# Three score units instead of two in a block of values, in the last two stretches of an attention and mixture-of-experts kernel

## The chip, the cores and the metric

The kernel runs on one core of one Trainium2 chip. The metric is the device time of one execution in microseconds (us). Three runs of the kernel before gave 296.19, 296.71 and 296.82 us: the median is 296.71 us. The execution that was profiled took 296.31 us, and its span, from the first to the last instruction, is 294.6 us.

## What is computed

The reference is one transformer layer on a single sequence, x of shape (1, 2048, 128) in fp32:

```python
x = x + _L0_attn_ref(_layernorm(x), w_qkv, w_out)
x = x + _L0_ffn_ref(_layernorm(x), base_W, base_b, shared_A, shared_B,
                    routed_A, routed_B, router_W, router_b)
```

The attention has 16 heads of 8 dimensions each, rotary embedding on queries and keys, a causal mask and a softmax over the keys:

```python
scores = jnp.einsum('bhqd,bhkd->bhqk', q, k) * scale
scores = jnp.where(causal, scores, jnp.finfo(scores.dtype).min)
out = jnp.einsum('bhqk,bhkd->bhqd', jax.nn.softmax(scores, axis=-1), v)
```

The feed-forward part adds a dense 128x128 layer, a shared low-rank pair (rank 16) and six routed low-rank pairs (rank 16), of which each token takes the two with the highest gate; the gates are a softmax over six logits, kept for those two and normalised again.

## The kernel before

**Stretches.** Queries are handled in six pieces of 2 or 4 tiles of 128 rows, `PIECES` = (0,2) (2,2) (4,4) (8,4) (12,2) (14,2), as (first tile, tiles). The text calls the time of a piece a stretch, numbered 0 to 5; the last two are stretches 4 and 5, each with 256 queries. In every stretch the 16 heads are taken in four groups of four, one group after the other.

**Score units.** The work of a group is a list of units, numbered through the whole kernel from 0 to 279. In a stretch of two tiles a unit is "wide" (one tile of 128 keys against 256 queries, four heads, 1024 scores in each of 128 partitions) or "half" (the last diagonal tile, 128 queries, 512 scores in a partition). The stretches begin at units 0, 8, 24, 76, 160 and 216. Stretch 4 has 14 units for each group and stretch 5 has 16, the last diagonal tile (the half unit) at the end of each group; only in the very last group the two diagonal tiles come first. So the half units of the last two stretches are 173, 187, 201, 215, 231, 247, 263 and 265.

For each unit TensorE computes the scores (L1198) into one of three slots of PSUM, `ps`; ScalarE takes the exponential of the whole slot (L758) into one of eight buffers in SBUF, `pbuf`; for diagonal units GpSimd sets the masked corner to zero (L685). The scores of unit n use the slot of unit n-3, so TensorE waits for the exponential of unit n-3 before them. The exponential of unit n waits until the block of values that reads the buffer of unit n-8 is done.

**Blocks of values.** The product of the exponentials with the values and a column of ones (L1223) is accumulated in one PSUM bank, `po`. `group_work` cuts the list of a group into blocks; a block's products are issued together, `LAG` = 5 units after its last unit. In stretches 4 and 5 a block is two wide or half units, and the last block of the kernel is cut into two of one unit. That makes 28 blocks in stretch 4 and 33 in stretch 5. After the last block of a group VectorE takes the sum out of `po` with a transpose (L831, `evacuate`), and the first block of the next group waits for that.

**Jobs.** All other work is cut into named jobs that are woven between the units: projections and splitting of queries and keys for later stretches, and the finish of a chunk of rows whose attention is done. The finish has eleven jobs: A (transpose), O (output projection and residual), M1 M2 M3 (layernorm), X (transpose), R (router and low-rank-down product), W1 W2 (choice of two routes), U (transpose of the gated low-rank rows), F (dense and up products, residual). O, X, R, U and F have a TensorE part (L1285, L1288, L1291, L1295, L1233 with L1299) and a VectorE part that reads it; R also has a small exponential on ScalarE (L766), which is placed in ScalarE's queue after the exponential of the unit that R is placed at, and waits for VectorE's logits (L984). U waits for VectorE's W2 and F for VectorE's copy of U. The chunks of rows are finished as c = 0 to 3 (4, 4, 4 and 2 tiles); the rows of the last two tiles are finished after the last unit by `end_of_chunk`.

**What sets the order.** Each engine has one queue in order, and the whole order is fixed by tables. `PLACES` gives, for each stretch, the unit (counted from the stretch's first) after whose scores each job comes. On TensorE the sequence at unit u is: the scores of u, the blocks of values that are due at u, the products placed at u. On VectorE it is: the evacuations due at u, the jobs placed at u. VectorE has no wait on a unit as such, so only the sequence of jobs and evacuations matters there. In stretches 0 and 1 the products of TensorE have places of their own (`SMALL_PLACES`), so `PLACES` moves only VectorE's jobs there. In what follows "O3 at 246" is the O product of chunk c = 3 placed at unit 246.

Of the kernel before, what the change touches and what calls it, by code (L numbers as in the profile page):

```python
# [73 lines left out]
NS_SMALL = 2  # L74
NPB = 8
LAG = 5


PREPS = ((0, 2), (2, 2), (4, 4), (8, 4), (12, 4))
PIECES = ((0, 2), (2, 2), (4, 4), (8, 4), (12, 2), (14, 2))  # L80
# [8 lines left out]
def group_work(t0, tiles, last):  # L89

    if tiles == 4:
        return ([[("full", kt, (0,)), ("full", kt, (1,))] for kt in range(t0 + 1)]
                + [[("ends", t0 + 1, (0,)), ("ends", t0 + 1, (1,))], [("mid", t0 + 2, (0, 1))]])
    wide = [("wide", kt, (0, 1)) for kt in range(t0 + 1)] + [("half", t0 + 1, (0, 1))]
    if last:
        wide = wide[-2:] + wide[:-2]
    return [wide[n:n + 2] for n in range(0, len(wide), 2)]


WOVEN = 1  # L100
# [7 lines left out]
def plan():  # L108


    units, blocks = [], []
    for i, (t0, tiles) in enumerate(PIECES):
        of_piece = []
        for g in range(NG):
            end = (i, g) == (NPIECE - 1, NG - 1)
            work = group_work(t0, tiles, end)
            if end:
                work[-1:] = [[unit] for unit in work[-1]]
            of_piece.append([(g, n, members, n == len(work) - 1) for n, members in enumerate(work)])
        if i == WOVEN:  # L120
            of_piece = [[one for both in zip(*of_piece[g:g + 2]) for one in both] for g in range(0, NG, 2)]
        for g, n, members, last in (one for group in of_piece for one in group):
            mine = list(range(len(units), len(units) + len(members)))
            for kind, kt, pairs in members:
                units.append(dict(i=i, g=g, kind=kind, kt=kt, pairs=pairs, diagonal=kt >= t0, block=len(blocks)))
            blocks.append(dict(i=i, g=g, units=mine, first=n == 0, last=last,
                               diagonal=any(units[u]["diagonal"] for u in mine)))
    return units, blocks
# [11 lines left out]
def blocks_by_unit():  # L140


    due = {}
    for b, block in enumerate(BLOCKS):
        due.setdefault(block["units"][-1] + LAG, []).append(b)
    return due


# [14 lines left out]
def value_terms(block):  # L163
# [49 lines left out]
    [(name, 2) for name in FINISH[FINISH_CUT:]] + [(name, 3) for name in FINISH],  # L213
)
PLACES = (
# [6 lines left out]
)  # L222


# [63 lines left out]
def build(nc, x, w_qkv, rope_c, rope_s, w_out, w_down, w_up, w_base, base_b, router_b, ident, head_sum,  # L288
# [3 lines left out]
    with ExitStack() as ctx:  # L292
# [487 lines left out]
        def _(dve):  # L780
# [384 lines left out]
            second_queries()  # L1165

            due = blocks_by_unit()
            for u in range(len(UNITS)):
                if u in FIRST_UNIT[1:] and FIRST_UNIT.index(u) in NEW_PREP:
# [4 lines left out]
                for n in JOBS_AT.get(u, ()):  # L1174
                    take(n)
            for u in range(len(UNITS), len(UNITS) + LAG):
                for b in due.get(u, ()):
# [5 lines left out]
        def _(pe):  # L1183
# [227 lines left out]
            pe.wait_ge(ones_set, 4)  # L1411
            pe.wait_ge(zeroed, 1)
            due = blocks_by_unit()
            for u in range(len(UNITS)):
                if u in FIRST_UNIT and FIRST_UNIT.index(u) in NEW_PREP:
# [13 lines left out]
                for name, c in PRODUCTS_AT.get(u, ()):  # L1429
                    job(name, c)  # L1430
            for u in range(len(UNITS), len(UNITS) + LAG):
                for b in due.get(u, ()):
# [59 lines left out]
```

## Time and profile before

| | us |
|---|---|
| median of three runs | 296.71 |
| profiled execution | 296.31 |
| its span | 294.6 |
| ScalarE busy | 268.9 (91%) |
| TensorE matmuls busy | 278.1 (94%) |
| VectorE busy | 138.6 (47%) |
| GpSimd busy | 65.5 (22%) |

The granted TensorE clock is at full speed (2.4 GHz) in every slice of the span. Instructions of ScalarE and TensorE are pipelined: a recorded duration can hold time in which the instruction waits behind the one before it, so a start is not always the true beginning, while an end is. For that reason this document counts with the ends of exponentials and with the distance from one matmul's start to the next one's start.

### The profile page before, as it was taken

How to read it: one execution, taken by the hardware profiler on the slowest of the kernel's cores; microseconds unless marked ns; L12 is line 12 of the kernel's file. 1: busy time of each engine (PE TensorE's matmuls, PEld its weight loads, DVE VectorE, ACT ScalarE, POOL GpSimd, SP SyncE). 2: the span in 40 equal slices, each digit the busy share in tenths (PEclk: the TensorE clock that was granted, in tenths of full speed). 3: DMA queues.
4: the chain of work that ended last, by engine and by line, in shares of the span. 5: the costliest groups of instructions: out<-in, count | busy, mean ns of one | idle time of the engine just before them, and what ended most of it. 6: DMA issues, size and time to landing. Idle time of an engine off the chain costs nothing.

```text
span 294.6 us, 7507 instructions
## 1 busy us (share of the span) xinstructions
PE 278.1 (94%) x2998; PEld 102.8 (35%) x2998; DVE 138.6 (47%) x419; ACT 268.9 (91%) x306; POOL 65.5 (22%) x139
## 2 busy tenths in 40 slices
PE   7979988999999999999999999999999999999996
PEld 2634332222222222132233134445433435444344
DVE  6875957686051558517171036522113262541055
ACT  8668899899999999999998999999999998999921
POOL 3647465423403021040030121010101010103002
PEclk9999999999999999999999999999999999999999
DMA  6343443004700000000001700001000000000000
GB/s 208 109 119 97 118 127 93 0 3 111 185 28 2 4 0 2 0 0 2 2 0 30 209 17 2 2 2 38 0 3 2 2 3 28 10 2 2 21 0 18
DMA packets 15400, 11.81 MB, mean 40 GB/s; under 512 B 2097, under 2 KB 14370, under 8 KB 15362
## 3 DMA queue, kind: packets, MB, share of 16 engines
q1 hardware_dynamic: 14738, 10.71, 13.1%
q8 instruction: 25, 0.41, 0.6%
q0 software_dynamic: 192, 0.39, 0.5%
q10 hardware_dynamic: 432, 0.20, 0.3%
q14 instruction: 13, 0.11, 0.1%
HBM read 3.95 MB, written 1.05 MB: 17 GB/s over the span
## 4 chain that ended last, share of the span: by engine, by line
PE 49%; ACT 26%; issue 14%; DVE 6%; DMA 2%; SPq 0%; ACTq 0%; DVEq 0%
ACT pbuf L758 26%; PE po L1223 22%; PE ps L1198 14%; PE pm L1239 1%; PE pm L1233 1%; PE pm L1285 1%; PE ps L1239 1%; PE ps L1347 1%; DMA qst<-parts 1%; PE pm L1245 1%; PE pm L1291 1%; PE pm L1299 1%; DMA xs<-x_dram 1%; DVE rest L851 1%; PE pm L1295 1%
## 5 line engine op out<-in xcount | busy, mean ns | idle before, releaser
L758 ACT ACTIVATE pbuf<-ps 128x1024 f32<-128x1024 f32 (+1 forms) x280 | 253.5, 1079 | 7.2 <-PE ps L1198 6.3
L1223 PE MATMUL po<-pbuf,va 128*9 128x256 f32 (+3 forms) x1792 | 143.8, 426 | 1.2 <-DVE oq L831 0.8
L1198 PE MATMUL ps<-qst,kst 64*128 64x256 bf16 (+3 forms) x896 | 97.3, 297 | 8.3 <-ACT pbuf L758 3.9
L685 POOL TENSOR_SCALAR_AFFINE_SELECT pbuf<-pbuf 128x256 f32<-128x256 f32 (+1 forms) x104 | 47.8, 482 | 194.1 <-ACT pbuf L758 193.7
L1198 PEld LDWEIGHTS ps<-qst,kst 64*128 64x128 bf16 x896 | 30.6, 94 | 106.8 <-ACT pbuf L758 80.3
L1223 PEld LDWEIGHTS po<-pbuf,va 128*9 128x9 f32 x1792 | 35.1, 89 | 55.4 <-issue 33.1
L831 DVE STREAM_TRANSPOSE oq<-po 128x256 f32<-128x256 f32 (+1 forms) x24 | 12.9, 539 | 66.4 <-PE po L1223 66.1
L851 DVE TENSOR_TENSOR rest<-pm,sinT 32x512 f32<-32x512 f32 x16 | 11.0, 687 | 0.3
L1347 PE MATMUL ps<-kst 128*128 128x512 bf16 (+1 forms) x38 | 9.8, 391 | 0.0
L798 DVE BATCH_NORM_STATS2 stats<-xs 128x6 f32<-128x128 f32 x32 | 7.1, 281 | 2.5 <-DMA xs<-x_dram 1.4
L1239 PE MATMUL ps<-xnT,wqkv 128*128 128x256 f32 (+1 forms) x24 | 8.0, 462 | 0.0
L999 DVE TENSOR_TENSOR xs<-pm,xs 128x512 f32<-128x512 f32 (+1 forms) x4 | 2.5, 624 | 11.1 <-PE pm L1299 11.1
L969 DVE TENSOR_TENSOR xs<-pm,xs 128x512 f32<-128x512 f32 (+1 forms) x4 | 2.5, 624 | 10.2 <-PE pm L1285 10.2
L1347 PE MATMUL ps<-xnT 128*128 128x512 bf16 x16 | 5.3, 508 | 1.5 <-DVE xnT L1129 1.5
L858 DVE TENSOR_TENSOR rot<-rot,rest 128x512 f32<-128x512 f32 (+1 forms) x10 | 6.4, 643 | 0.3
L996 DVE COPY lowT<-pm 113x512 f32<-113x512 f32 (+1 forms) x4 | 2.5, 625 | 8.5 <-PE pm L1295 8.5
L960 DVE COPY va<-pm 128x512 f32<-128x512 f32 x2 | 1.4, 692 | 10.8 <-PE pm L1245 10.8
L981 DVE TENSOR_TENSOR lg<-pm,rbias 128x24 f32<-128x24 f32 (+1 forms) x4 | 0.7, 180 | 12.1 <-PE pm L1291 12.1
L845 DVE TENSOR_TENSOR rot<-pm,cosT 128x512 f32<-128x512 f32 x4 | 2.8, 691 | 7.5 <-PE pm L1239 6.9
L634 POOL MEMSET qst<- 128x512 f32 (+1 forms) x9 | 6.0, 686 | 0.0
L701 ACT COPY kst<-fillers 128x2048 f32<-128x2048 f32 x3 | 5.7, 1897 | 0.0
L977 DVE COPY feat<-pm 128x512 f32<-128x512 f32 (+1 forms) x4 | 2.5, 625 | 6.4 <-PE pm L1288 6.4
(158 smaller groups left out, 189.5 us busy)
## 6 DMA issues: line engine op xcount, KB each, us to landing
qst<-parts SPq DMA_DIRECT2D x18, 128.0 KB, 2.6
kst<-parts SPq DMA_DIRECT2D x18, 128.0 KB, 2.4
xs<-x_dram SPq DMA_DIRECT2D x4, 256.0 KB, 3.2
cosT<-rope_c_dram SPq DMA_DIRECT2D x3, 256.0 KB, 3.8
sinT<-rope_s_dram SPq DMA_DIRECT2D x3, 256.0 KB, 4.1
out_dram<-xs SPq DMA_DIRECT2D x3, 256.0 KB, 2.3
kst<-parts SPq DMA_DIRECT2D x8, 64.0 KB, 2.4
qst<-parts SPq DMA_DIRECT2D x7, 64.0 KB, 2.0
```

Of the source, the lines that this page charges most:

```text
L634: nc.gpsimd.memset(stacked[:, :, first * P:(first + tiles) * P].bitcast(F32), value).then_inc(filled_by_pool, 1)
L685: ins = nc.gpsimd.affine_select(out=edge, in_=edge, compare_op=ALU.is_ge, fill=0.0, base=0, pattern=[[0, edge.shape[1]], [1, P]], channel_ ...
L701: nc.scalar.copy(kst[:, :, c * CH:(c + 1) * CH].bitcast(F32), fillers[:, 0:1].unsqueeze(2).broadcast_to([P, NP, CH // 2])).then_inc(filled, 1)
L758: nc.scalar.activation(probs[:, :, 0:width], ps[:, SLOT[u], :, 0:width], ACT.Exp, scale=SCALE).then_inc(exp_ready, 1)
L798: ins = nc.vector.bn_stats(stats[:, t, :], xs[:, tile + t, :])
L831: nc.vector.transpose(oq[:, g, mine, :].rearrange("p b r -> p (b r)"), po[:, output(i, g, 0, nt * P)]).then_inc(o_free, 1)
L851: ins = nc.vector.tensor_tensor(rest[there:there + HALF, which, cols], product[here:here + HALF, :], sinT[here:here + HALF, c % 2, cols], ...
L858: return nc.vector.tensor_tensor(rot[:, which, cols], rot[:, which, cols], rest[:, which, cols], ALU.add)
L1198: ins = nc.tensor.matmul(ps[:, SLOT[u], e, place:place + n], side(kst, e)[:, g * 2 + pair, key:key + P], side(qst, e)[:, g * 2 + pair, q:q ...
L1223: ins = nc.tensor.matmul(po[32 * j:32 * j + DH + 1, output(i, g, q0, n)], va[:, kt, g * GH + j, :], pbuf[:, u % NPB, at:at + n], start=blk ...
L1239: return nc.tensor.matmul(product, wqkv[:, which, :], xnT[:, chunk(p) % 2, local(p)], start=True, stop=True)
L1347: nc.tensor.matmul(into, left, right, start=True, stop=True)
```

## The change

A block of values in stretches 4 and 5 has up to three units in place of two; it is still issued five units after its last unit (the new `WIDE_LAG` has the value of `LAG`). That makes 20 blocks in stretch 4 (three, three, three, three and two units in each group) and 24 in stretch 5 (five of three units and one of one unit in each group). The last block of the kernel is then one unit, and the one before it three.

The places of jobs are changed in four of the six stretches. In stretch 0, K1 goes from 1 to 0, and in stretch 1, Q1 goes from 1 to 2. In stretch 4, W1 of chunk 1 goes from 24 to 27. In stretch 5 the finish of chunk 2 has W1, W2, U and F three units earlier, and the finish of chunk 3 has A, M1, M2, M3, X, R, W1, W2, U and F one to four units earlier; O stays. The products of TensorE that move are U2 (240 to 237), F2 (243 to 240), X3 (254 to 251), R3 (257 to 254), U3 (267 to 263) and F3 (270 to 266).

```diff
@@ -74,6 +74,8 @@
 NS_SMALL = 2
 NPB = 8
 LAG = 5
+WIDE_LAG = 5
+WIDE_BLOCK = 3
@@ -94,7 +96,8 @@
     wide = [("wide", kt, (0, 1)) for kt in range(t0 + 1)] + [("half", t0 + 1, (0, 1))]
     if last:
         wide = wide[-2:] + wide[:-2]
-    return [wide[n:n + 2] for n in range(0, len(wide), 2)]
+    size = 2 if t0 < 12 else WIDE_BLOCK
+    return [wide[n:n + size] for n in range(0, len(wide), size)]
@@ -142,7 +145,7 @@
     due = {}
     for b, block in enumerate(BLOCKS):
-        due.setdefault(block["units"][-1] + LAG, []).append(b)
+        due.setdefault(block["units"][-1] + (WIDE_LAG if PIECES[block["i"]][0] >= 12 else LAG), []).append(b)
     return due
@@ -213,12 +216,12 @@
 PLACES = (
-    (0, 0, 0, 1, 5),
-    (0, 1, 1, 3, 6, 6, 7, 11, 15, 15),
+    (0, 0, 0, 0, 5),
+    (0, 1, 2, 3, 6, 6, 7, 11, 15, 15),
     (6, 9, 10, 11, 12, 18, 22, 23, 25, 30, 34, 37, 40),
     (3, 3, 5, 8, 11, 19, 26, 31, 34, 34, 35, 39, 40, 44, 46, 50, 50, 51, 54, 61, 61, 62, 68, 72),
-    (7, 8, 10, 10, 12, 17, 19, 24, 27, 27, 33, 37, 40),
-    (3, 6, 9, 11, 15, 18, 21, 24, 27, 30, 30, 31, 35, 36, 38, 41, 44, 48, 51, 54),
+    (7, 8, 10, 10, 12, 17, 19, 27, 27, 27, 33, 37, 40),
+    (3, 6, 9, 11, 15, 15, 18, 21, 24, 27, 30, 30, 32, 33, 35, 38, 41, 45, 47, 50),
 )
```

## Rows read from the trace of the kernel before

**Rows 1.** Stretch 5: window, length, busy of PE PEld DVE ACT POOL, clock, DMA
```profile
222.80:281.40 58.60, 57.01 (x828) 25.47 (x823) 21.31 (x81) 56.86 (x65) 5.46 (x13) 1.00 0.03 9
```
**Rows 2.** ScalarE's timeline, units 150 to 279: start, length to last end, what
```profile
161.24 27.42 ACT L758 ACTIVATE pbuf<-ps 128x1024 f32<-128x1024 f32 x30 [0.28 <-PE ps L1198]
...
188.99 12.48 ACT L758 ACTIVATE pbuf<-ps 128x1024 f32<-128x1024 f32 x14
201.81 1.03 ACT L758 ACTIVATE pbuf<-ps 128x1024 f32<-128x1024 f32 x1 [0.34 <-PE ps L1198]
203.12 32.99 ACT L758 ACTIVATE pbuf<-ps 128x1024 f32<-128x1024 f32 x37 [0.28 <-PE ps L1198]
236.39 0.22 ACT L766 ACTIVATE gate<-lg 128x24 f32<-128x24 f32 x1 [0.28 <-DVE lg L984]
236.52 11.08 ACT L758 ACTIVATE pbuf<-ps 128x1024 f32<-128x1024 f32 x12
248.35 1.02 ACT L758 ACTIVATE pbuf<-ps 128x1024 f32<-128x1024 f32 x1 [0.75 <-PE ps L1198]
249.65 11.94 ACT L758 ACTIVATE pbuf<-ps 128x1024 f32<-128x1024 f32 x13 [0.28 <-PE ps L1198]
...
261.49 11.26 ACT L758 ACTIVATE pbuf<-ps 128x1024 f32<-128x1024 f32 x13
272.97 8.36 ACT L758 ACTIVATE pbuf<-ps 128x1024 f32<-128x1024 f32 x9 [0.23 <-PE ps L1198]
```
**Rows 3.** ScalarE's timeline, units 213 and 215 (half), each in a narrow window
```profile
219.33 1.14 ACT L758 ACTIVATE pbuf<-ps 128x1024 f32<-128x1024 f32 x1
...
221.13 0.74 ACT L758 ACTIVATE pbuf<-ps 128x512 f32<-128x512 f32 x1
```
**Rows 4.** TensorE's timeline at units 243 to 246: F2, scores, values
```profile
245.93 1.16 PE L1233 MATMUL pm<-wbase,feat 128*128 128x128 f32 x8
...
247.91 0.39 PE L1198 MATMUL ps<-qst,kst 64*128 64x256 bf16 x4
248.23 1.05 PE L1223 MATMUL po<-pbuf,va 128*9 128x256 f32 x16
249.22 0.61 PE L1198 MATMUL ps<-qst,kst 64*128 64x256 bf16 x8
249.76 1.05 PE L1223 MATMUL po<-pbuf,va 128*9 128x256 f32 x16
```
**Rows 5.** TensorE's timeline: the scores of unit 216 wait for unit 213
```profile
220.52 0.39 PE L1198 MATMUL ps<-qst,kst 64*128 64x256 bf16 x4 [0.24 <-ACT pbuf L758]
```
**Rows 6.** TensorE's timeline: X1 and R2, each with the scores after it
```profile
184.97 0.66 PE L1288 MATMUL pm<-idf,ln 128*128 128x128 f32 x4
185.55 0.39 PE L1198 MATMUL ps<-qst,kst 64*128 64x256 bf16 x4
...
234.52 1.15 PE L1291 MATMUL pm<-wdown,feat 128*128 128x118 f32 x8
235.61 0.39 PE L1198 MATMUL ps<-qst,kst 64*128 64x256 bf16 x4
```
**Rows 7.** TensorE's timeline: the last values and the first matmuls of the end
```profile
279.35 2.78 PE L1223 MATMUL po<-pbuf,va 128*9 128x256 f32 x48
282.06 1.25 PE L1347 MATMUL ps<-kst 128*128 128x512 bf16 x5
```
**Rows 8.** VectorE's timeline: evacuation, end of W2 of chunk 2; evacuation in stretch 1
```profile
239.95 0.45 DVE L831 STREAM_TRANSPOSE oq<-po 128x256 f32<-128x256 f32 x1 [1.26 <-PE po L1223]
...
241.99 0.56 DVE L993 TENSOR_TENSOR low_rank<-low_rank,gate 128x384 f32<-128x384 f32 x1
...
30.24 0.45 DVE L831 STREAM_TRANSPOSE oq<-po 128x256 f32<-128x256 f32 x1
```
**Rows 9.** Queries of stretch 2: SyncE stacks them, TensorE's first scores use them
```profile
29.57 4.78 SPq L573 DMA_DIRECT2D qst<-parts  x6
...
42.29 0.60 PE L1198 MATMUL ps<-qst,kst 64*128 64x512 bf16 x4
```

## The prediction

> **What bounds the kernel now.** I read the busy times by stretch first. In stretch 5 both TensorE (57.0 of 58.6 us) and ScalarE (56.9) are marked busy for 97% of the time [rows 1], and stretch 4 is alike, which doesn't say which of them holds the other. ScalarE's timeline does. In an undisturbed run of nine wide exponentials the ends are (8.36 - 1.02) / 8 = 0.917 us apart; 1.02 us is what one takes when nothing is ahead of it [rows 2]. A half unit takes about 0.49: unit 213 ends at 220.47, so unit 214 at 221.39, and unit 215, a half, at 221.87 [rows 3]. From the end of unit 150 (162.26) to the end of unit 279 (281.33) there are 121 wide and 8 half steps, 121 x 0.917 + 8 x 0.49 = 114.9 us of 119.07. So ScalarE sets the pace, and 4.2 us are stalls. The ends of the runs [rows 2] put them, by the product behind which they stand, at O1 0.23, R1 0.40, F1 0.83, O2 0.24, R2 0.49, F2 1.23, O3 0.34, R3 0.09, F3 0.32. Not one stands where TensorE has only scores and values. (R2 as an example: the run before ends at 236.11, the one behind at 247.60, 12 steps, 11.49 - 11.00.)
>
> **The rule by which I count.** Write p(n) for the start of unit n's scores on TensorE and E(n) for the end of its exponential.
> - p(n) is at least E(n-3) + 0.06: the scores of unit 216 start at 220.52, unit 213 ended at 220.47 [rows 3, 5].
> - Scores to next scores 0.21, scores to values or a product 0.32 (247.91 to 248.23, and 0.54 for two) [rows 4]; half-unit scores 0.1 less, an estimate (half the columns).
> - A block of two (V2) 0.98: 248.23 to 249.22 [rows 4]. Six units back to back took 279.35 to 282.06 = 2.71 [rows 7]. So a wide unit is 0.43 and a change from values back to scores 0.12; a block of three (V3) is 1.41, and a half unit in a block 0.21. The added unit's price is read from this slope, since no V3 is in the trace.
> - Products: F2 1.98 [rows 4], R2 1.09 and X1 0.58 [rows 6]. By estimate O1 and O2 are 1.09 (as many matmuls as R), U1 and U2 0.59 (as X), and those of chunk 3 half plus 0.05 to 0.1 (F3 1.09, U3 0.37, O3 0.64).
> - E(n) is the later of E(n-1) + 0.917 (0.49 if half) and p(n) + 1.45: 247.91 to 248.35, and 1.02 [rows 2, 4]. Behind R the small exponential waits for logits: R2's product ends at 235.61, the gate starts at 236.39 (+0.78), and the exponential behind ends at 247.60 - 11 x 0.917 = 237.51 (+1.12) [rows 2, 6]; I take +1.93 in all from R's end.
>
> With blocks of two this rule gives 4.0 us of stalls at the same products as the trace's 4.2, so I trust it to a few tenths.
>
> **Part 1: three units in a block.** In the steady state nothing stalls, before or after. Behind V3, p(n) = E(n-4) + 0.06 + 0.32 + 1.41 = E(n-3) + 0.87; on time is E(n-3) + 2.75 - 1.45 = 1.30. The slack is 0.43 us behind a V3 where it was 0.86 behind a V2. What is saved: 17 blocks fewer (61 to 44), each with 0.11 + 0.12 us of change between scores and values, 3.9 us of TensorE's time. That is time of an engine that doesn't set the pace; it pays only where a product has put TensorE behind. What is lost: the half of the slack into which a product had to fit.
>
> *A page of the Trainium skill speaks for the change here.* The rows show that each pair of changes costs 0.23 us [rows 4, 7]. The Trainium skill, TensorEngine Tiling (Array Packing), section Key Properties, says that a change of tiling mode drains TensorE; scores use 64-row tiles and values narrow column tiles, so this is where such a drain would lie. The trace agrees that there is a cost. If that drain were what the pace hangs on, the time would fall by up to 3.9 us; that is the first rival below.
>
> **Part 2: where products meet V3.** By the rule, with the order behind each unit taken from the tables (reference point in brackets):
> - F2 at 240, V3 at 239 (E(236)): p(239) = 0.06, p(240) = 1.79, p(241) = 1.79 + 0.32 + 1.98 = 4.09; E(241) = 5.54 where 5 x 0.917 = 4.58 was due: 0.95, and 0.11 behind the next V3. 1.06, in place of 1.23.
> - F3 at 266, between U3 at 263, V3 at 264 and V3 at 267 (E(258)): p(263) = 2.00, p(264) = 2.59, p(265) = 4.32, p(266) = 4.43, p(267) = 5.84, p(268) = 7.57; E(268) = 9.02, and due is 7 x 0.917 + 2 x 0.49 + 0.917 = 8.32, for both 263 and 265 are half units, in which ScalarE runs ahead: 0.7 and some 0.2 from smaller delays before, 0.91 in place of 0.32.
> - R1 at 179 (E(173)): V3 at 176, X1 at 177, V2 with a half at 178: p(177) = 1.79, p(178) = 2.70, p(179) = 3.79, R ends at 5.19, + 1.93 = 7.12, due 6.42: 0.70 in place of 0.40.
> - U1 at 187, now behind a V3 (E(184)): p(188) = 0.06 + 0.22 + 1.41 + 0.59 = 2.28; E(188) = 3.73, due 3.24: 0.48, where there was none.
> - R2 at 231, V3 at 229 and 232: 0.58 in place of 0.49. O2 at 200, V3 at 201 (E(197)): p(202) = 3.10, 4.55 against 4.16: 0.38 in place of 0.24.
> - O1 0.17 for 0.23. F1 at 193 (a V2 with a half ahead of it): 0.42 for 0.83. O3 none for 0.34, as V3 at 245 stands a unit ahead. R3 the same 0.09. U2, X3 and U3 none of their own.
>
> Sum after: 4.8 us, against 4.0 by the same rule and 4.2 in the trace: 0.6 to 0.8 longer; I take +0.7. For the bounds: each term rests on estimates of 0.1; with every meeting better by 0.1 it is -0.3, with each worse and a wait more, +1.6.
>
> Waits on VectorE. U2 now comes right behind W2. Before, an evacuation stood between W1, which ended at 239.95 - 1.26 = 238.69, and W2, which ended at 242.55 [rows 8]. W2 is one operation of 0.56 and five of about 0.2 (an estimate), 1.6 in all; without the evacuation ahead of it, it ends at 240.3, 4.7 us behind R2's end (235.61). TensorE reaches U2 some 4.6 behind R2's end: p(237) = E(234) + 0.06. So U2 is just covered, and I count 0; if W2 gained nothing the wait would be 2.3, less the slack of 0.4 to 0.9, which is an upper bound of 1.9. Behind U2 on TensorE stand the scores of unit 238. Evacuations gain a unit: the first block of a group is now issued seven units behind its start, not six.
>
> **Part 3: the end.** Before, the last values run without a gap from 279.35 to 282.06 [rows 7], 0.73 after ScalarE's last end, 281.33 [rows 2]. After (E(274)): p(277) = 0.06, V3, p(278) = 1.79, p(279) = 2.00, V3 from 2.32 to 3.61; the next V3 needs unit 278 and starts at 3.73, to 5.02; the last unit to 5.45; the end's matmuls at 5.57, 0.98 after E(279) = 4.59. That is 0.25 us later against the trace, 0.37 against the rule's own 0.61 for before. I take +0.3, between them; bounds 0 (the block in time) and +0.45 (a unit's values). Everything behind, 13 us of it, moves with it.
>
> **Part 4: stretches 0 and 1.** K1 passes no evacuation and no job: VectorE's queue is the same. Q1 of chunk 2 now comes behind an evacuation of 0.45 us [rows 8]; SyncE's six stacking DMAs start later by that, from 29.57, and their end is set by the third part of the queries, whose place is unchanged; they are used at 42.29 [rows 9]. I count 0, with 0 to +0.45 above if that cover is gone, and -0.2 if an earlier evacuation helps.
>
> **Sum.** +0.7 + 0.3 + 0 = +1.0 us. On the profiled execution 296.31 to 297.3. The median of the runs, 296.71, is 0.40 above it; with the same distance it is 297.7 us.
>
> **Rivals.**
> - *TensorE is the bound, and fewer changes pay* (faster). For it: 97% busy, 4.2 us of stalls behind products, 3.9 us less work for the same engine. Against it: the pace of 0.917 is ScalarE's, and the trace has no stall away from a product. If half of the stalls beyond the three gates' 0.3 go, -1.95, less the end's 0.3: 296.71 - 1.65 = 295.1. It decides if stalls behind F1, F2 and O3 vanish and none arises at 188 and 268. Chance 0.14.
> - *A draw*: stalls change places only, as F1 and O3 gain 0.75 and R1, U1 and F3 lose less than I count, and the end's V3 runs in time. 296.7, within 0.2% (0.6 us, about what a measurement of this kernel can tell from no change). Chance 0.20.
> - *V3 breaks the slack everywhere*: buffers of `pbuf` come free three at a time, and the exponential eight units on waits for the block. By the rule V3 ends 1.9 after E(n-3), due is 2.65. If it took 0.8 more, all of some 38 blocks would stall, 0.05 us each at first: +1.9 beside the 1.0, 299.6. Chance 0.06.
> - *My forecast*, slower by 0.3 to 2 us: 0.60.
>
> Of the forecast's chance 0.05 lies within 0.2%. So faster 0.14, same 0.20 + 0.05 = 0.25, slower 0.55 + 0.06 = 0.61. The likeliest case's own range is 297.0 to 298.6; over all cases it is 295.9 to 298.8.
>
> **What would show it.** ScalarE's timeline: a stall of about 0.5 at unit 188, about 1 at 241, 0.8 at 268, none at 247 and 249, steps of 0.917 elsewhere; stalls over stretches 4 and 5 of 4.8 to 5. V3 of 24 matmul records and 1.41 us to the next scores. The end's first matmul 1.0 us after the last exponential. It is wrong if units 188 and 268 come on time, if V3 costs less than 1.3, or if the stalls fall below 4 us.

## The result, and the profile after

The changed kernel takes 297.56 us (median of 8 runs, 297.36 to 298.14) where the kernel before takes 296.61 (median of 8). The ratio is 1.0041, with a 95% interval of 1.0032 to 1.0050: the medians are 0.95 us apart, and the ratio puts the difference at 1.2 us (0.95 to 1.5). The profiled execution of the changed kernel has a span of 295.9 us against 294.6. The forecast was 297.7 us, slower than before.

All lines of the code after the tables are three further down in the changed kernel: L761 is the exponential, L1201 the scores, L1226 the values.

ScalarE's timeline of the kernel after, units 150 to 279 (start, length to the last end, what), to be set beside [rows 2]:

```profile
161.39 27.38 ACT L761 ACTIVATE pbuf<-ps 128x1024 f32<-128x1024 f32 x30 [0.27 <-PE ps L1201]
...
189.40 6.99 ACT L761 ACTIVATE pbuf<-ps 128x1024 f32<-128x1024 f32 x8
196.81 5.60 ACT L761 ACTIVATE pbuf<-ps 128x1024 f32<-128x1024 f32 x6 [0.42 <-PE ps L1201]
202.63 7.13 ACT L761 ACTIVATE pbuf<-ps 128x1024 f32<-128x1024 f32 x8 [0.22 <-PE ps L1201]
210.06 26.75 ACT L761 ACTIVATE pbuf<-ps 128x1024 f32<-128x1024 f32 x30 [0.29 <-PE ps L1201]
...
237.22 8.47 ACT L761 ACTIVATE pbuf<-ps 128x1024 f32<-128x1024 f32 x9
246.56 12.74 ACT L761 ACTIVATE pbuf<-ps 128x1024 f32<-128x1024 f32 x14 [0.86 <-PE ps L1201]
...
259.28 11.30 ACT L761 ACTIVATE pbuf<-ps 128x1024 f32<-128x1024 f32 x13
271.30 11.10 ACT L761 ACTIVATE pbuf<-ps 128x1024 f32<-128x1024 f32 x12 [0.71 <-PE ps L1201]
```

What to look for is where the runs break: at units 188 (196.81), 194 (202.63), 202 (210.06), 241 (246.56) and 268 (271.30). At 188 the end of the run before is 196.39 and the first end behind is 196.81 + 1.02 = 197.83, 1.44 where 0.917 is due: a stall of 0.52 at a place that had none before. At 268 it is 272.32 - 270.58 - 0.917 = 0.82, where the kernel before had 0.33 at 271. From the end of unit 150 (162.41) to that of unit 279 (282.40) it is 119.99 us, against 119.07 [rows 2]: 0.92 us longer for the same exponentials.

TensorE's timeline of the kernel after, around F2 at 240, to be set beside [rows 4]:

```profile
244.14 1.16 PE L1236 MATMUL pm<-wbase,feat 128*128 128x128 f32 x8
...
246.12 0.61 PE L1201 MATMUL ps<-qst,kst 64*128 64x256 bf16 x8
246.66 1.48 PE L1226 MATMUL po<-pbuf,va 128*9 128x256 f32 x24
248.08 0.86 PE L1201 MATMUL ps<-qst,kst 64*128 64x256 bf16 x12
```

The block of three has 24 records and takes 1.42 us to the next scores (246.66 to 248.08); the prediction had 1.41 from a slope. Behind it stand three units of scores in a row (x12), where blocks of two had at most two. F2 takes 1.98 us (244.14 to 246.12), as before.

The end of the loop in the kernel after, to be set beside [rows 7]:

```profile
279.61 0.61 PE L1201 MATMUL ps<-qst,kst 64*128 64x256 bf16 x8
280.15 3.30 PE L1226 MATMUL po<-pbuf,va 128*9 128x256 f32 x56
283.38 0.82 PE L1350 MATMUL ps<-kst 128*128 128x512 bf16 x3
```

Seven units of values (56 records) are left behind the last scores, not six, and the first matmul behind them comes 283.38 - 282.40 = 0.98 us after the last exponential, against 0.73 before. That matmul (`keep_warm` in the kernel) computes nothing that is used, so it is only a sign of the end of the values. What the finish hangs on is VectorE's transpose of the last sum, first of the kernel before, then of the kernel after:

```profile
282.26 0.45 DVE L831 STREAM_TRANSPOSE oq<-po 128x256 f32<-128x256 f32 x1 [9.12 <-PE po L1223]
```

```profile
283.59 0.45 DVE L834 STREAM_TRANSPOSE oq<-po 128x256 f32<-128x256 f32 x1 [10.91 <-PE po L1226]
```

It starts 0.93 us after the last exponential before (282.26 - 281.33) and 1.19 after (283.59 - 282.40), 0.26 later.

Where did the saved changes go? The two windows below run from the scores of unit 160 to the first matmul behind the last values, first in the kernel before, then in the kernel after; the first columns are the window, its length and the busy time of TensorE's matmuls:

```profile
169.42:282.06 112.64, 109.88 (x1573) 48.68 (x1573) 39.15 (x139) 109.25 (x125) 12.52 (x28) 1.00 0.03 9
```

```profile
169.47:283.39 113.92, 107.30 (x1573) 50.45 (x1573) 39.68 (x139) 109.53 (x125) 12.47 (x28) 1.00 0.03 9
```

The matmuls are the same 1573 records. They keep TensorE busy 2.58 us less, not the 3.9 that 17 blocks fewer at 0.23 us would give. The order of the records says why: TensorE leaves its scores for other work 70 times in the window before and 58 times in the window after, 12 fewer. Where a block is gone from ahead of a product, TensorE changes from scores to the product all the same. Twelve changes there and back at 0.23 are 2.8 us. The 2.6 us saved were not lost elsewhere on TensorE: its idle time in the window grew from 2.8 to 6.6 us, by the 2.6 and by the 1.3 that the window is longer, and 6.0 of the 6.6 are waits for ScalarE to free a slot.

### The profile page after: what moved, and what is told of

The parts are those of the page before. It is cut to its first block, busy times and chain, and to the rows that moved or that the text cites. A ratio compares the mean times of both kernels' runs of the same rounds, so it can differ in the third digit from the quotient of the medians.

```text
span 295.9 us, 7508 instructions
## 1 busy us (share of the span) xinstructions
PE 275.6 (93%) x2998; PEld 104.6 (35%) x2998; DVE 139.0 (47%) x419; ACT 269.1 (91%) x306; POOL 65.5 (22%) x139
## 4 chain that ended last, share of the span: by engine, by line
PE 48%; ACT 26%; issue 14%; DVE 10%; DMA 1%; ACTq 0%; DVEq 0%
ACT pbuf L761 26%; PE po L1226 21%; PE ps L1201 13%; PE ps L1350 2%; PE pm L1242 1%; PE pm L1288 1%; PE pm L1236 1%; PE ps L1242 1%; PE pm L1294 1%; PE pm L1248 1%; PE pm L1302 1%; DMA xs<-x_dram 1%; DVE stats L801 1%; DVE rest L854 1%; DVE xn L491 1%
## 5 line engine op out<-in xcount | busy, mean ns | idle before, releaser
L761 ACT ACTIVATE pbuf<-ps 128x1024 f32<-128x1024 f32 (+1 forms) x280 | 253.7, 1063 | 7.5 <-PE ps L1201 6.8
L1226 PE MATMUL po<-pbuf,va 128*9 128x256 f32 (+3 forms) x1792 | 140.9, 426 | 1.0 <-DVE oq L834 0.8
L1201 PE MATMUL ps<-qst,kst 64*128 64x256 bf16 (+3 forms) x896 | 95.7, 297 | 11.9 <-ACT pbuf L761 8.7
L1201 PEld LDWEIGHTS ps<-qst,kst 64*128 64x128 bf16 x896 | 30.9, 94 | 107.2 <-ACT pbuf L761 78.9
L1226 PEld LDWEIGHTS po<-pbuf,va 128*9 128x9 f32 x1792 | 36.6, 89 | 54.7 <-issue 29.7
L694 POOL TENSOR_TENSOR ln<-xs,ln 128x128 f32<-128x128 f32 x2 | 0.9, 454 | 21.5 <-ACT ln L780 21.5
```

Of the source, the lines that this page charges most:

```text
L761: nc.scalar.activation(probs[:, :, 0:width], ps[:, SLOT[u], :, 0:width], ACT.Exp, scale=SCALE).then_inc(exp_ready, 1)
L1201: ins = nc.tensor.matmul(ps[:, SLOT[u], e, place:place + n], side(kst, e)[:, g * 2 + pair, key:key + P], side(qst, e)[:, g * 2 + pair, q:q ...
L1226: ins = nc.tensor.matmul(po[32 * j:32 * j + DH + 1, output(i, g, q0, n)], va[:, kt, g * GH + j, :], pbuf[:, u % NPB, at:at + n], start=blk ...
```

## Experiments

Eleven kernels were run. The theory is that of the prediction: ScalarE sets the pace, and what costs is the time by which a block of values and a product together overrun the slack of three score slots. For each kernel two numbers are read from the trace beside its time: *pace*, from the end of unit 159's exponential to the end of unit 279's, and *end*, from there to the end of the last instruction. "Stall" is a step between two ends less 0.917 (0.493 for a half unit). The kernel before has a pace of 110.81 and an end of 13.23 us, the kernel after 111.74 and 13.48. Each kernel is compared with runs of the kernel before on the same chip, whose medians were 296.61 us (for the kernel after), 296.36 (e1, e2, e4, e5), 296.31 (e3, e8, e9, e10) and 296.31 (e7, e11, e12). The kernels from e4 on are built from the changed kernel and keep its early places, which e3 shows to be worth nothing. The diffs show the lines that matter; a comment behind a line gives the value of `WIDE_BLOCK` in that kernel.

| kernel | pace | end | median us | ratio to before (95%) |
|---|---|---|---|---|
| after | 111.74 | 13.48 | 297.56 | 1.0041 (1.0032 to 1.0050) |
| e1_blocks_only | 112.39 | 13.48 | 297.98 | 1.0054 (1.0041 to 1.0067) |
| e2_places_only | 112.37 | 13.23 | 297.80 | 1.0048 (1.0035 to 1.0061) |
| e3_early_only | 110.82 | 13.22 | 296.35 | 0.9994 (0.9974 to 1.0013) |
| e4_f3_late | 110.96 | 13.48 | 296.83 | 1.0018 (1.0010 to 1.0027) |
| e5_last_group_two | 111.75 | 13.23 | 297.59 | 1.0037 (1.0025 to 1.0049) |
| e7_four_lag4 | 121.47 | 13.70 | 307.77 | 1.0388 (1.0370 to 1.0405) |
| e8_two_replaced | 110.33 | 13.23 | 295.84 | 0.9979 (0.9959 to 1.0000) |
| e9_two_split | 108.79 | 13.23 | 294.06 | 0.9915 (0.9887 to 0.9943) |
| e10_three_split | 110.61 | 13.48 | 296.39 | 0.9995 (0.9977 to 1.0014) |
| e11_one_old_places | 119.75 | 13.73 | 305.98 | 1.0328 (1.0311 to 1.0345) |
| e12_two_lag4 | 114.34 | 13.11 | 299.96 | 1.0126 (1.0109 to 1.0143) |

**Is it the blocks or the places?** Two kernels take the change apart. The first has the blocks of three and every job at its old place.

```diff
-    return [wide[n:n + 2] for n in range(0, len(wide), 2)]
+    size = 2 if t0 < 12 else WIDE_BLOCK        # 3
+    return [wide[n:n + size] for n in range(0, len(wide), size)]
```

> Blocks of three as in the changed kernel, every job at its old place. My theory (a block of three halves the slack behind it, and the cost lies where products meet such a block): by the rule of the prediction, worked through unit by unit, stalls of 5.3 us where before has 4.0 by the same rule, a last stall group at unit 244 of 1.1, a stall of 0.5 at 249, 0.4 at 268, and 0.26 more at the end: 1.6 us over before, 298.2 us (297.7 to 298.7). Rival (the blocks pay, the new places cost): 296.6 or less. Rival (places do nothing): 297.6, as the changed kernel.

The second has blocks of two and the new places of stretches 4 and 5.

```diff
-    (7, 8, 10, 10, 12, 17, 19, 24, 27, 27, 33, 37, 40),
-    (3, 6, 9, 11, 15, 18, 21, 24, 27, 30, 30, 31, 35, 36, 38, 41, 44, 48, 51, 54),
+    (7, 8, 10, 10, 12, 17, 19, 27, 27, 27, 33, 37, 40),
+    (3, 6, 9, 11, 15, 15, 18, 21, 24, 27, 30, 30, 32, 33, 35, 38, 41, 45, 47, 50),
```

> Blocks of two as before, the jobs of the last two stretches at the new places. My theory: the new places suit blocks of three; with blocks of two they collide: stalls of 1.4 at 241 (U2 waits for W2, then F2), 0.9 at 255, 0.7 at 267; 5.3 us of stalls in all, end unchanged: 1.4 us over before, 298.0 us (297.3 to 298.5). Rival (the new places alone make the changed kernel slower): 297.6. Rival (the blocks alone do): 296.6.

Measured: 1.6 us and 1.4 us over before. By pace and end the two are 1.83 and 1.56 us over it, and the whole change is 1.18, so each part alone is slower than the whole; their times alone, whose intervals overlap, would not show that. Blocks of three alone have the stalls of 1.13 at 244, 0.49 at 249 and 0.42 at 268 that were expected, and one of 0.43 at 256, where TensorE waits 1.00 us for VectorE's layernorm ahead of X3. The places alone, with blocks of two, have 1.58 at 241, 0.95 at 255 and 0.77 at 267. The rival that the blocks pay falls, for blocks of three alone are slower than before. That the new places are the culprit can't be told from the time of the second kernel, which lies near that rival's 297.6; it falls because the stalls of this kernel are others than those of the changed one, and because the same places shorten the pace of blocks of three by 0.65 us. ScalarE's timeline of the kernel with new places only:

```profile
246.83 12.80 ACT L758 ACTIVATE pbuf<-ps 128x1024 f32<-128x1024 f32 x14 [1.47 <-PE ps L1198]
260.37 0.21 ACT L766 ACTIVATE gate<-lg 128x12 f32<-128x12 f32 x1 [0.75 <-DVE lg L984]
```

The first line waits 1.47 us for the scores of unit 241; the second is the exponential of R3, which waits 0.75 for its logits.

**The early places.** K1 and Q1 alone.

```diff
-    (0, 0, 0, 1, 5),
-    (0, 1, 1, 3, 6, 6, 7, 11, 15, 15),
+    (0, 0, 0, 0, 5),
+    (0, 1, 2, 3, 6, 6, 7, 11, 15, 15),
```

> The kernel before with only K1 (stretch 0) and Q1 (stretch 1) at their new places. My theory: VectorE's queue changes by one swap, Q1 behind an evacuation of 0.45 us, which is covered on both sides: no difference to before, within 0.1% (296.2 to 296.8 where before has 296.5). Rival (SyncE's stacking of the queries starts later and holds stretch 2): 0.3 to 0.5 us longer, with the first scores of stretch 2 later in the trace.

No difference: 296.35 against 296.31, pace and end as before. VectorE's timeline of that kernel, to be set beside [rows 8], and the first scores of stretch 2, to be set beside [rows 9]:

```profile
28.85 0.45 DVE L831 STREAM_TRANSPOSE oq<-po 128x256 f32<-128x256 f32 x1
29.33 0.43 DVE L866 CAST parts<-rot 128x512 bf16<-128x512 f32 x1
...
42.27 0.61 PE L1198 MATMUL ps<-qst,kst 64*128 64x512 bf16 x4
```

The evacuation stands ahead of Q1's cast now, the cast is 0.28 later than in the kernel before (29.05), and the scores that need these queries start at 42.27, as before (42.29). This part of the change is worth nothing.

**One place alone.** The largest term of the loss by the prediction was F3 at 266. The changed kernel with that one number put back:

```diff
-    (3, 6, 9, 11, 15, 15, 18, 21, 24, 27, 30, 30, 32, 33, 35, 38, 41, 45, 47, 50),
+    (3, 6, 9, 11, 15, 15, 18, 21, 24, 27, 30, 30, 32, 33, 35, 38, 41, 45, 47, 54),
```

> The changed kernel with one entry of the table altered: F3 back at unit 270. My theory: F3 at 266 meets a block of three at 267 just behind the half units 263 and 265; at 270 it stands a unit ahead of one and has 0.14 of stall in place of 0.93 at 267 and 268: 0.8 us less than the changed kernel, 296.8 us (296.4 to 297.1). Rival (TensorE's backlog is what counts, a product costs the same wherever it stands in the last group): 297.5, as the stall moves to 271 to 273.

Measured: 296.83 us, 0.73 less than the changed kernel, and a pace 0.78 shorter (expected 0.8). The stalls of 0.13 and 0.82 at 267 and 268 are gone, and one of 0.15 at 272 has come. First the kernel after, from the scores of 265 and 266, then this kernel, from those of 269 and 270:

```profile
267.60 0.50 PE L1201 MATMUL ps<-qst,kst 64*128 64x128 bf16 x8
268.03 0.71 PE L1236 MATMUL pm<-wbase,feat 128*128 128x128 f32 x4
268.58 0.61 PE L1302 MATMUL pm<-wup,lowT 113*128 113x128 f32 x4
269.12 0.39 PE L1201 MATMUL ps<-qst,kst 64*128 64x256 bf16 x4
269.45 1.48 PE L1226 MATMUL po<-pbuf,va 128*9 128x256 f32 x24
270.86 0.39 PE L1201 MATMUL ps<-qst,kst 64*128 64x256 bf16 x4
```

```profile
270.32 0.61 PE L1201 MATMUL ps<-qst,kst 64*128 64x256 bf16 x8
270.86 0.71 PE L1236 MATMUL pm<-wbase,feat 128*128 128x128 f32 x4
271.41 0.61 PE L1302 MATMUL pm<-wup,lowT 113*128 113x128 f32 x4
271.95 0.39 PE L1201 MATMUL ps<-qst,kst 64*128 64x256 bf16 x4
272.28 1.27 PE L1226 MATMUL po<-pbuf,va 128*9 128x256 f32 x24
273.48 0.84 PE L1201 MATMUL ps<-qst,kst 64*128 64x256 bf16 x12
```

F3's matmuls take the same 1.09 us in both. In the first they come behind two half units (64x128 in the scores of 265), through which ScalarE ran in 0.49 us each, and the block of three behind them (1.41, all wide) is met with the slack used up; in the second there are only wide units around, and the block (1.20, with one half unit) costs nearly nothing. So the same product costs 0.95 or 0.15 us by its place alone, and the rival, that TensorE's backlog costs the same anywhere in the group, falls.

**The end alone.** The changed kernel with the last group in blocks of two.

```diff
-    size = 2 if t0 < 12 else WIDE_BLOCK
+    size = 2 if t0 < 12 or last else WIDE_BLOCK
```

> The changed kernel with the last group (units 264 to 279) in blocks of two and its last block in two of one unit, as before. My theory: the stalls are the same, 0.8 at 268 included, and from the end of the last exponential to the end of the span it is 13.18 us again, as before, not 13.43: 0.25 us less than the changed kernel, 297.3 us. Rival (the end follows the last exponential whatever the blocks): no difference, 13.43 again.

The trace has it as expected: the stalls are those of the changed kernel to 0.01, and the end is 13.23 and not 13.48, so the rival falls. TensorE's timeline of this kernel at the end, to be set beside that of the kernel after (56 records there) and [rows 7]:

```profile
280.68 2.78 PE L1226 MATMUL po<-pbuf,va 128*9 128x256 f32 x48
283.62 0.59 PE L1350 MATMUL ps<-kst 128*128 128x512 bf16 x2 [0.16 <-issue]
```

The matmul behind the values comes 0.95 us after the last exponential (283.62 - 282.67), almost as late as in the kernel after, and the end is 0.25 shorter all the same: VectorE's transpose starts 0.93 after that exponential, as in the kernel before. So the end goes by the last values and their transpose, not by that matmul.

The time doesn't show the 0.25 us: 297.59 against 297.56 us, from different groups of runs whose kernel before differed by 0.25. A part so small is below what such medians can tell apart, and it rests on the traces.

**The size of a block, at fixed places.** One unit, five behind, old places:

```diff
+    size = 2 if t0 < 12 else WIDE_BLOCK        # 1
```

> Blocks of one unit in stretches 4 and 5, five units behind it, jobs at the places of the kernel before. Against before (two) and the kernel with blocks of three at the old places this gives the size alone. My theory: the slack behind a block of one is larger still, but each unit now pays the change of 0.23 us, TensorE has 0.21 + 0.11 + 0.43 + 0.12 = 0.87 us of work for each 0.917 of ScalarE, so that nothing is left to make up for a product: by the rule stalls of 11.4 us where before has 4.0, and the end 0.5 longer, 8 us over before, 304.3 us (303 to 306). Rival (smaller blocks are always better, as the slack behind them is greater): under 296.3.

Blocks of two and of four, four units behind, old places (`WIDE_LAG` = 4; `WIDE_BLOCK` = 2 or 4):

> Blocks of two, issued four units behind their last unit in place of five, old places (stretches 4 and 5 only; the early swap of Q1 is in). My theory: by the rule the values start no earlier than before in the free case but meet the products at other units, at 180, 194, 244, 256, 258: stalls of 7.3 us where before has 4.0, 3.3 us over before, 299.6 us (298.5 to 300.5). Rival (the lag doesn't matter while five buffers are enough): 296.3.

> Blocks of four units, issued four units behind the last (with five, the exponential eight units on would wait for the block), old places. My theory: behind a block of four the slack is 0.43 - 0.43 = 0, so each product near one is a stall of its full length: stalls of 13.3 us by the rule, and 6 us over blocks of two with the same lag, 306 us (303.5 to 307.5). Rival (the change pays once TensorE has fewer changes, 30 blocks fewer than with two save 6 us of its time): at or under the kernel with blocks of two and lag 4.

With the lag of five and the same places in stretches 4 and 5, one, two and three units give 305.98, 296.31 and 297.98 us; with the lag of four, two and four units give 299.96 and 307.77. For one and for four units the forecast was right in sign and 1.7 and 1.8 us too small (8 for 9.7, 6 for 7.8), and the 307.77 lies outside its range. TensorE's timeline of the kernel with blocks of one:

```profile
225.69 0.39 PE L1201 MATMUL ps<-qst,kst 64*128 64x256 bf16 x4
226.01 0.62 PE L1226 MATMUL po<-pbuf,va 128*9 128x256 f32 x8
226.56 0.39 PE L1201 MATMUL ps<-qst,kst 64*128 64x256 bf16 x4
```

Then TensorE's timeline of the kernel with blocks of four, and ScalarE's in the same stretch:

```profile
233.21 1.91 PE L1226 MATMUL po<-pbuf,va 128*9 128x256 f32 x32
235.05 0.66 PE L1291 MATMUL pm<-idf,ln 128*128 128x128 f32 x4
235.64 0.83 PE L1201 MATMUL ps<-qst,kst 64*128 64x256 bf16 x12
```

```profile
226.29 9.29 ACT L761 ACTIVATE pbuf<-ps 128x1024 f32<-128x1024 f32 x10 [0.34 <-PE ps L1201]
236.07 3.35 ACT L761 ACTIVATE pbuf<-ps 128x1024 f32<-128x1024 f32 x4 [0.50 <-PE ps L1201]
```

With one unit, scores and values alternate every 0.87 us (225.69, 226.56), which leaves hardly anything of ScalarE's 0.917, so that a long product is paid almost in full (the stall behind F2 is 1.86 us, its length 1.98). With four, a block takes 1.85 us to the next scores. A block alone holds nothing up: the block before this one runs from 229.52 to 231.37, inside ScalarE's unbroken run from 226.29 to 235.58. This one has X2 behind it (0.59 us, 235.05 to 235.64), and the exponential after it is 0.60 late: the slack is used up by the block, and the product is paid in full.

Neither pair shows the size of a block alone, for VectorE's work has a part in both. With one unit, TensorE waits eight times, 3.3 us in all, for VectorE's evacuation ahead of the first values of a group, since these are due one unit behind the last values of the group before. With the lag of four, TensorE waits for VectorE's layernorm ahead of X3, 1.47 us with blocks of two and 2.49 with blocks of four, and the stalls behind it, at 255 and 256, are 0.86 and 3.68 us: 2.8 of the 7.2 us by which the stalls of the two kernels differ. The lag matters too: one unit less costs 3.65 us at size two.

**Better places for blocks of two.** By the same rule, worked through unit by unit, other places were found for the jobs of stretches 4 and 5.

```diff
+    (3, 9, 9, 15, 20, 24, 33, 36, 39, 39, 46, 52, 53),
+    (4, 15, 15, 15, 21, 23, 29, 29, 35, 36, 39, 42, 44, 44, 44, 47, 48, 51, 52, 55),
```

> Blocks of two, with the jobs of stretches 4 and 5 placed anew so that products stand away from half units and from each other. My theory (blocks of two have the greater slack, and the places were not the best for them): by the rule stalls of 2.5 us where before has 4.0, end unchanged: 1.4 us under before, 295.1 us (294.6 to 295.8). Rival (only fewer changes between scores and values can win more time here): no gain over before, 296.5 or more.

A third of the forecast gain, and just outside its range: 295.84 us, 0.5 under before, with an interval that reaches no change. The pace is 110.33, where 1.4 less than before would be 109.4, and the stalls are 3.75 us and not 2.5. The largest are at F1 (207: 0.92) and F2 (252: 0.66), and behind them, in chunk 3, at 257 (0.39), R3 (264: 0.47), U3 (269: 0.49) and F3 (273: 0.36). In that chain jobs are packed tight: TensorE waits 0.80 us for VectorE ahead of U3, and 0.19 for an evacuation just before 257. A wait on VectorE that the rule had too short is the likely cause of the excess there; no kernel isolates it.

**Shorter products.** The dense half of F needs only VectorE's copy of X, and may be issued ahead of the half that needs U, once U has been read out of the bank that they share (`...` marks lines left out):

```diff
+BASE_AHEAD = {0: 3, 1: 3, 2: 3, 3: 1}
...
                 elif name == "F":
-                    base(product, nt)
+                    if c not in BASE_AHEAD:
+                        base(product, nt)
...
+                for c in BASES_AT.get(u, ()):
+                    pe.wait_ge(job_fed, FED[AWAITED["F", c]])
+                    base(pm[:, :], FINISHES[c][1])
```

> Blocks of two, jobs of stretches 4 and 5 placed anew, and the dense product of F issued one to three units ahead of its other half, for all four chunks, so that no job of TensorE is longer than 1.09 us; F0 also goes two units later in stretch 3. My theory: by the rule stalls in stretches 4 and 5 of 1.6 us where before has 4.0, and some 0.8 of the 1.0 at units 149 and 150 in stretch 3 goes: 3.1 us under before, 293.4 us (292.8 to 294.4). Rival (backlog counts, not the length of one product): the gain of e8 only, 295.1.

> As e9_two_split, with blocks of three and places found for blocks of three by the same rule. My theory (the slack behind a block decides, not the changes saved): stalls in stretches 4 and 5 of 2.85 us against 1.6 for blocks of two, and the end 0.26 longer: 1.5 us over e9_two_split, 294.9 us (294.3 to 295.6). Rival (with places of their own, blocks of three win by the 3.9 us of changes that they save): at or under e9_two_split.

Blocks of two with split products take 294.06 us, 2.25 under before: the fastest kernel here. Its stalls in stretches 4 and 5 are 2.2 us where before had 4.25. TensorE's timeline of this kernel around F1, and ScalarE's in the last part:

```profile
202.61 1.16 PE L1244 MATMUL pm<-wbase,feat 128*128 128x128 f32 x8
203.70 0.39 PE L1209 MATMUL ps<-qst,kst 64*128 64x256 bf16 x4
204.02 1.05 PE L1234 MATMUL po<-pbuf,va 128*9 128x256 f32 x16
205.00 0.61 PE L1209 MATMUL ps<-qst,kst 64*128 64x256 bf16 x8
205.54 1.05 PE L1234 MATMUL po<-pbuf,va 128*9 128x256 f32 x16
206.53 1.16 PE L1311 MATMUL pm<-wup,lowT 113*128 113x128 f32 x8
```

```profile
249.80 13.55 ACT L769 ACTIVATE pbuf<-ps 128x512 f32<-128x512 f32 x15 [0.57 <-PE ps L1209]
...
263.19 16.00 ACT L769 ACTIVATE pbuf<-ps 128x1024 f32<-128x1024 f32 x18
```

The two halves (1.09 us each) have three units of scores and two blocks of values between them, and from 249.80 on ScalarE's runs break only for R3's small exponential. The time is in the forecast range but 0.7 over its middle, 293.4, mostly by stretch 3, where I had worked nothing out unit by unit: with F0 two units later there are stalls of 0.33, 0.17 and 0.38 at 148 to 152 where I had counted on 0.2 in all. Against e8 this kernel has split products and other places at once, so that what the split alone is worth isn't shown.

Blocks of three with split products and places of their own take 296.39 us, no faster than before, 2.3 over blocks of two and outside the forecast range (294.9; 294.3 to 295.6). Their stalls are 4.07 us, where 2.85 were expected. TensorE waits on VectorE there for U2 (0.40 us) and R3 (0.57), while the kernel with blocks of two has no such wait over 0.15 us. The rival, that blocks of three win once they have places of their own, falls further than expected for these places; but the places come from the same kind of search by the same rule, not from one that tried all of them, so that the best kernel of either size isn't known.

Of the four comparisons made, the larger blocks lost three (three against two at the old places, three against two with split products, four against two with the lag of four). In the fourth, at the places made for three, they have the shorter pace (111.74 against 112.37) and the longer end (13.48 against 13.23), and the times (297.56 and 297.80) are too close to tell apart.

## Why the prediction was right

**The bound.** ScalarE sets the pace: away from the listed units the ends stay 0.917 us apart, in the kernel after as before.

**Place by place.** Stalls in us, forecast by the prediction and read from the ends of the exponentials:

| product | forecast | after | before |
|---|---|---|---|
| O1 | 0.17 | 0.21 | 0.23 |
| R1 | 0.70 | 0.72 | 0.40 |
| U1 | 0.48 | 0.53 | 0 |
| F1 | 0.42 | 0.45 | 0.83 |
| O2 | 0.38 | 0.40 | 0.24 |
| R2 | 0.58 | 0.63 | 0.49 |
| F2 | 1.06 | 1.10 | 1.23 |
| O3 | 0 | 0 | 0.34 |
| X3 | 0 | 0.10 | 0 |
| R3 | 0.09 | 0.10 | 0.09 |
| F3 | 0.91 | 0.95 | 0.32 |
| sum | 4.8 | 5.2 | 4.2 |

Each is within 0.05 but for X3, which I had at none: its product starts 0.16 us later than the block of values ahead of it lets it, at the end of VectorE's layernorm. The step of the sum was named +0.7, chosen between +0.6 and +0.8, and is +0.92. The mechanism is right place by place; the size is a little small, because nearly every place is 0.01 to 0.05 over the rule and because of X3, 0.4 us in all, where the rule's total for before is only 0.2 under the trace. The new U1 stall stands where it should, behind a block of three:

```profile
194.34 1.48 PE L1226 MATMUL po<-pbuf,va 128*9 128x256 f32 x24
195.75 0.69 PE L1298 MATMUL pm<-idf,low_rank 128*113 128x128 f32 x4
196.37 0.83 PE L1201 MATMUL ps<-qst,kst 64*128 64x256 bf16 x12
```

Values from 194.34, U1 from 195.75, and the scores of unit 188 only at 196.37, 0.44 ahead of its exponential at 196.81.

**The end.** Forecast 0.98 us after the last exponential for the first matmul, measured 0.98; the step was +0.3 and is +0.25. As a sign of it that matmul served by luck: in e5 the same matmul comes at 0.95 with the end of the kernel before. What moves the end is the last values, which are 0.25 later, as the prediction's sum had them.

**The changes saved.** The prediction had 3.9 us of TensorE's time saved, worth nothing. It was worth nothing, and it is 2.6 us and not 3.9: the count of blocks was taken for the count of changes (17 for 12). The Trainium skill, TensorEngine Tiling (Array Packing), section Key Properties, says that a change of tiling mode drains TensorE. The traces agree that a change costs, 0.11 us into the values and 0.12 out of them in blocks of one, two, three and four (0.55, 0.98, 1.42 and 1.85 us to the next scores); whether that cost is such a drain, no run here shows. Fewer changes pay only so far as TensorE is what the pace hangs on, and the kernel with a change behind each unit (e11) is close to that.

**U2 behind W2, stretches 0 and 1.** W2 ended 4.96 us behind R2's matmuls, where 4.7 was forecast, and U2 waited 0.15 us for it; the slack covered that, and no stall came at 238. The early places gave 0, as counted.

**The sum.** By the traces +0.92 + 0.25 = +1.17 us; timed, +0.95 between the medians and +1.2 (0.95 to 1.5) by the ratio. The forecast +1.0 is inside, a little under what the traces show. That 297.56 lies so close to 297.7 is in part luck: the median of before was 296.71 when the forecast was made and is 296.61 over eight runs, and the difference of the medians is at the low end of the interval.

The rival of a gain fell because the stalls at 188 and 268 arose and those behind F1 (0.45) and F2 (1.10) stayed, as its own condition had it. The draw fell with them: F1 and O3 gain 0.7, as it said, but R1, U1 and F3 lose 1.5. The slack of `pbuf` never broke, since outside the products the steps stay at 0.917.

## What to carry to other kernels

Where one engine sets the pace and another feeds it through a few slots, the mean load of the feeder says little: what counts is the longest stretch of other work between two feeds, against the lead that the slots give. Merging small pieces of work saves changes on average and spends that lead; splitting the longest piece gives some of it back, and was worth 2.25 us here together with new places. In stretches 4 and 5 blocks of two ran best at the places made for two, and blocks of three better at the places made for three, so size and places are to be changed, and judged, together. And merged pieces save only the changes that go: where other work stands behind a removed piece, the change stays.

## What the runs showed of the hardware

Recorded durations of ScalarE's exponentials grow from 1.02 us to as much as 1.36 in an undisturbed run, while their ends stay 0.917 apart: only the ends can be used for counting. Stalls at the same units agreed to 0.01 us between kernels that share the code up to there (0.08, 0.13, 0.73, 0.53, 0.33 at units 169 to 194 in the kernel after, e1, e4 and e5), far closer than the medians of their times, which move by 0.3 us; a part of the change as small as 0.25 us could be told in the trace and not in the time.
